# The lead-in of an mLSTM and FFN layer with its roundings on GpSimd and low gate weights last, and the turns of g and h later from chunk 4 on

## The reference

```python
h  = recurrence(layernorm(x) @ W + b)            # W is 256 x 1024: gates i, f, o and z
x1 = x + h / rms(h) * scale
u  = layernorm(x1)
out = x1 + u + 0.5 * (silu(layernorm_affine(u) @ w1 + b1) @ w2 + b2)
```

## Time and profile before

| | |
|---|---|
| time, median of 3 runs | 321.24 us (321.14 to 321.33) |
| the profiled execution | 321.89 us, span 320.0 us |
| busy share of the span | PE 95%, PEld 82%, DVE 84%, ACT 72%, POOL 37% |
| TensorE clock granted, mean | 0.989 of full speed |
| DMA | 13.12 MB on the main queue, 11.8% of 16 engines' span |

### The profile page before, as it was taken

One profiled execution on the slowest core, in us unless ns is written; L12 is line 12 of the kernel. 1 busy time (PEld: TensorE's weight loads), 2 busy tenths in 40 slices (PEclk: granted clock), 3 DMA queues, 4 the chain that ended last, 5 costly groups with the idle time before them and its releaser, 6 DMA issues.

```text
span 320.0 us, 4813 instructions
## 1 busy us (share of the span) xinstructions
PE 303.9 (95%) x1760; PEld 263.8 (82%) x1760; DVE 267.4 (84%) x474; ACT 229.7 (72%) x372; POOL 118.1 (37%) x126
## 2 busy tenths in 40 slices
...
GB/s 274 357 374 14 1 0 2 0 0 0 2 1 2 33 98 3 34 98 2 1 2 33 98 0 2 33 36 0 1 2 25 43 0 0 68 0 5 63 0 68
DMA packets 10951, 14.21 MB, mean 44 GB/s; under 512 B 688, under 2 KB 10160, under 8 KB 10672
## 3 DMA queue, kind: packets, MB, share of 16 engines
q1 hardware_dynamic: 10512, 13.12, 11.8%
q10 hardware_dynamic: 416, 0.79, 0.7%
...
## 4 chain that ended last, share of the span: by engine, by line
PE 45%; DVE 20%; issue 14%; POOL 12%; ACT 6%; DMA 3%; POOLq 0%; DVEq 0%; SPq 0%
PE mm_ps L221 7%; PE mm_ps L219 7%; PE mm_ps L220 7%; PE z_ps L220 6%; PE z_ps L219 6%; PE z_ps L221 6%; POOL rows L1034 3%; DVE rec L672 2%; DVE g L729 2%; DMA rows<-x 2%; POOL rec L1001 2%; DVE rows L737 2%; POOL g L1019 2%; DVE bn L742 2%; DVE rec L687 2%
## 5 line engine op out<-in xcount | busy, mean ns | idle before, releaser
L219 PE MATMUL z_ps<-w_hi,y_hi 128*128 128x256 f32 x248 | 71.3, 288 | 1.4 <-issue 1.4
L220 PE MATMUL z_ps<-w_lo,y_hi 128*128 128x256 f32 x248 | 70.4, 284 | 0.0
L221 PE MATMUL z_ps<-w_hi,y_lo 128*128 128x256 f32 x248 | 70.4, 284 | 0.0
L765 DVE TENSOR_TENSOR y_lo<-y,y_hi 128x512 fp32r<-128x512 f32 x64 | 43.2, 687 | 12.2 <-ACT y_hi L504 11.7
L501 ACT ACTIVATE y<-mm_ps,b_all 128x512 f32<-128x512 f32 x60 | 41.3, 688 | 13.4 <-PE mm_ps L288 9.8
L219 PEld LDWEIGHTS z_ps<-w_hi,y_hi 128*128 128x128 f32 x248 | 47.5, 191 | 1.9 <-issue 1.8
L220 PEld LDWEIGHTS z_ps<-w_lo,y_hi 128*128 128x128 f32 x248 | 47.2, 190 | 0.1
L221 PEld LDWEIGHTS z_ps<-w_hi,y_lo 128*128 128x128 f32 x248 | 47.1, 190 | 0.0
L1005 POOL TENSOR_TENSOR rrms<-meansq,minus_half 128x4 f32<-128x4 f32 x8 | 9.0, 1122 | 96.5 <-DVE meansq L723 96.5
L219 PE MATMUL mm_ps<-gt_hi,w_hi 128*128 128x512 f32 x108 | 43.2, 400 | 0.0
L220 PE MATMUL mm_ps<-gt_lo,w_hi 128*128 128x512 f32 x108 | 42.8, 396 | 0.0
...
## 6 DMA issues: line engine op xcount, KB each, us to landing
...
```

Of the source, the lines that this page charges most:

```text
L219: pe.matmul(dst, wh[w_at], ah[a_at], start=start, stop=False)
L220: pe.matmul(dst, wh[w_at], al[a_at], start=False, stop=False)
L221: return pe.matmul(dst, wl[w_at], ah[a_at], start=False, stop=stop)
L765: dve.tensor_tensor(y_lo[:, j], y[:, j % YBUFS], y_hi[:, j].bitcast(F32), ALU.subtract).then_inc(y_lo_done, 1)
```

## The change

The diff, cut to its core:

```diff
@@ @block.tensor
...
+            def first_two_gates():
+
+                x_hi, x_lo = xt(0)
+                f = [slice(GATE_ORDER[j] * P, GATE_ORDER[j] * P + P) for j in range(2)]
+                for k in range(KD):
+                    pe.wait_ge(wg_split_hi, k + 1)
+                    pe.wait_ge(xt_hi_done, k + 1)
+                    for j in range(2):
+                        pe.matmul(gate_bank(0, j), wg_hi[:, k, f[j]], x_hi[:, k], start=(k == 0), stop=False)
+                for k in range(KD):
+                    pe.wait_ge(xt_lo_done, k + 1)
+                    for j in range(2):
+                        pe.matmul(gate_bank(0, j), wg_hi[:, k, f[j]], x_lo[:, k], start=False, stop=False)
+                pe.wait_ge(wg_split_lo, KD)
+                for j in range(2):
+                    for k in range(KD):
+                        ins = pe.matmul(gate_bank(0, j), wg_lo[:, k, f[j]], x_hi[:, k], start=False,
+                                        stop=(k == KD - 1))
                     ins.then_inc(pre_done, 1)
...
-            gates(0, range(0, 5))
+            first_two_gates()
+            gates(0, range(2, 6))
             x_turned(1)
-            gates(0, range(5, GJ))
-            gates(1, range(0, 7))
+            gates(0, range(6, GJ))
+            gates(1, range(0, 5))
             x_turned(2)
-            gates(1, range(7, GJ))
-            gates(2, range(0, 2))
+            gates(1, range(5, GJ))
+            gates(2, range(0, 1))
             h_turned(0)
-            gates(2, range(2, GJ))
+            gates(2, range(1, GJ))
...
             for t in range(4, CHUNKS - 1):
                 gates(t, range(GJ))
+                fc2(t - 3, range(0, 2))
                 g_turned(t - 2)
-                fc2(t - 3, range(0, 2))
+                fc2(t - 3, range(2, TT))
                 x_turned(t + 1)
-                fc2(t - 3, range(2, TT))
+                fc1(t - 2, range(0, 2))
                 h_turned(t - 1)
-                fc1(t - 2, range(KF))
+                fc1(t - 2, range(2, KF))
             gates(7, range(GJ))
+            fc2(4, range(0, 2))
             g_turned(5)
-            fc2(4, range(TT))
+            fc2(4, range(2, TT))
...
@@ @block.scalar
-            act.preload_act_table_set("sigmoid_and_others")
+            act.preload_act_table_set("exp_and_others")
...
-            act.wait_ge(bias_ready, 3)
+            act.wait_ge(bias_ready, 5)
+
 
             gates(0, I_TILES)
-            act.preload_act_table_set("natural_log_exp_and_others")
             exp_i(0)
             act.preload_act_table_set("sigmoid_and_others")
-            gates(0, F_TILES)
+            gates(0, range(2, 6))
             x_high(1)
-            gates(0, range(4, 7))
-            act.wait_ge(w1_scaled, 1)
-            act.activation(w1_hi[:, 1], w1_f[:, 1], ACT.Copy).then_inc(w1_rounded, 1)
-            gates(0, range(7, GJ))
             x_normalised(2)
+            gates(0, range(6, GJ))
...
             gates(3, range(0, 1))
             square_sums(1)
-            gates(3, range(1, 4))
-            act.wait_ge(w2_scaled, 1)
-            act.activation(w2_hi[:], w2_f, ACT.Copy).then_inc(w2_rounded, 1)
-            gates(3, range(4, GJ))
+            gates(3, range(1, 2))
+            act.preload_act_table_set("sigmoid_and_others")
+            gates(3, range(2, GJ))
...
@@ @block.vector
-            for k in range(KD):
-                dve.wait_ge(wg_split_hi, k + 1)
-                dve.tensor_tensor(wg_lo[:, k], wg_raw[:, k], wg_hi[:, k].bitcast(F32), ALU.subtract
-                                  ).then_inc(wg_split_lo, 1)
...
+            dve.tensor_scalar(gate_bias[:, 2:4], col[:, 2:4], -1.0, None, ALU.mult).then_inc(bias_ready, 1)
+            dve.tensor_copy(gate_bias[:, 4:6], col[:, 6:8]).then_inc(bias_ready, 1)
+            dve.tensor_copy(gate_bias[:, 6:8], col[:, 4:6]).then_inc(bias_ready, 1)
+
+            ln1_sums(1)
             x_low(0)
...
-            dve.wait_ge(w1_scaled, 1)
-            dve.tensor_copy(w1_hi[:, 0], w1_f[:, 0]).then_inc(w1_rounded, 1)
             maximum(0, range(KD))
+            input_times_z(0)
             x_low(1)
...
-            y_low(0, range(2, 4))
-            for j in range(4, KF):
-                y_high(0, j)
-                y_low(0, range(j, j + 1))
-
-            ln1_sums(4)
+            y_low(0, range(2, KF))
+
+            ln1(4)
             mean_square(1)
-            ln1_means(4)
-            h_scaled(1)
             dve.wait_ge(w2_rounded, 1)
             dve.tensor_tensor(w2_lo[:], w2_f, w2_hi[:].bitcast(F32), ALU.subtract).then_inc(w2_ready, 1)
+            h_scaled(1)
             residual(1)
...
@@ @block.gpsimd
+            def y_high(c, j):
+                pool.wait_ge(silu_done, at(c, 8, j + 1))
+                pool.tensor_copy(y_hi[:, j], y[:, j % YBUFS]).then_inc(y_hi_done, 1)
+
...
             ln1_root(0)
+            for k in range(KD):
+                pool.wait_ge(wg_split_hi, k + 1)
+                pool.tensor_tensor(wg_lo[:, k], wg_raw[:, k], wg_hi[:, k].bitcast(F32), ALU.subtract
+                                   ).then_inc(wg_split_lo, 1)
             ln1_root(1)
             ln1_root(2)
-            input_times_z(0)
+            pool.wait_ge(w1_scaled, 1)
+            pool.tensor_copy(w1_hi[:], w1_f).then_inc(w1_rounded, 1)
...
             ln2_root(0)
             ln1_root(3)
+            for j in range(4, KF):
+                y_high(0, j)
+            pool.wait_ge(w2_scaled, 1)
+            pool.tensor_copy(w2_hi[:], w2_f).then_inc(w2_rounded, 1)
+            ln1_root(4)
             rms_root(1)
-            ln1_root(4)
             ln2_root(1)
```

More of the change, by code:

```diff
@@ L530, in _ @@
             exp_i(1)
+            x_high(2)
             act.preload_act_table_set("sigmoid_and_others")
[L532 to L536 removed]
+            gates(1, range(2, GJ))
+            gates(2, range(0, 1))
             square_sums(0)
[L538 removed]
+            gates(2, range(1, GJ))
             g_normalised(0)
@@ L875, in _ @@
             divisor(2)
-            numerators(2)
+            numerators(2, range(0, 1))
             g_low(1)
+            numerators(2, range(1, KD))
             newton(2)
```

122 lines of the change are left out of this document (68 added, 54 removed).

## The result

The changed kernel takes 325.78 us (324.85 to 326.67, 4 runs), the kernel before 321.19: a ratio of 1.0118, 95% interval 1.0092 to 1.0144. By that ratio it is slower by 1.2%; the two medians lie 4.6 us apart. I had forecast 318.0 and a range up to 320.9. The profiled execution took 326.67 us, 4.8 more than that of before (321.89), with a span of 324.6.

A forecast was written before the change was run, and what follows sets the result against it. PE (busy 95%) bounds the kernel, plus its waits and half-clock stretches. 0 to 90 us, +0.7 (to 1.5), -4.45 and 0 to +0.4 give -3.75 to -2.6, taken as -3.2: 318.0 us, range 315.6 to 320.9.

The forecast's parts named there:

- the lead-in's +0.4: Start of the kernel: POOL's wg_lo delays the first gate_bias and xt_lo, so PE comes 0.4 us later.
- rival C: Lead-in: POOL's wg_lo holds up DVE's scalings of chunk 0's x, once (320.4) or twice (322.8); chance 0.12.
- the 0 for the end of chunk 0's FFN: Up to 90 us: the 2.3 gained at fc2(0) is given back waiting at g_turned(1), sum about 0.
- 14 to 56 us, -1.15: Waits of 0.44 (xt_hi) and 0.72 (g of chunk 0) go; with the +0.4, PE is 0.75 earlier at fc1(0).
- POOL's rounding, 1.84: End of chunk 0's FFN: POOL's cast of w2 takes 1.84 us, between bounds of 1.68 and 3.24.
- The chain to g_turned(1): Chunk 0's FFN end: root stands behind w2_lo, g(1) is late, PE waits 2.25 us; half clock up to +1.7 possible.
- the 2.3: fc2(0) starts at 79.05 instead of 81.32 through earlier w2_lo: -2.3, counting the 0.75.
- Chunk 2's turn of h, +0.7: At h_turned(2), x_low(4) on a DVE 0.9 late delays PE: +0.7, with a fallen clock +1.5.
- Step 4, -4.45: Loop at t = 4: fc2 tiles ahead of g_turned(2) remove waits of 0.53 and 2.21 and the half clock (1.7).
- Steps 5 and 6, 0: Loop at t = 5 and 6: PE waited for nothing and g_high and g_low stay early enough: 0.
- Behind the loop I had 0 to +0.4: End of the kernel: a small remainder of 0 to +0.4 us.

The follow-up runs named there:

- first run: The kernel before with one edit, wg_lo subtracted by POOL at the place the changed kernel has it: 325.50 us, ratio 1.0130.
- third run: The changed kernel with POOL waiting for the four scalings of chunk 0's x before it subtracts wg_lo: 326.15 us, ratio 1.0148.
- thirteenth run: The changed kernel with wg_lo on DVE, x_low(0) right behind it, and the end of chunk 0's FFN as before: 320.22 us, ratio 0.9954.
- 2: The changed kernel with wg_lo subtracted by DVE right after x_normalised(0), as before: 324.47 us, ratio 1.0089.
- 5: The changed kernel with wg_lo on DVE and x_low(0) directly behind it, ahead of gate_bias and chunk 1's statistics: 323.99 us, ratio 1.0075.
- 6: The kernel before with the new loop, plus the changed kernel's end of chunk 0's FFN alone: 322.68 us, ratio 1.0024.
- 14: The changed kernel with shifted_bias in four pieces between tiles of gates(2) and g_normalised(0) earlier on ACT: 326.05 us, ratio 1.0144.
- the fourth: The kernel before with only the new order of the loop from t = 4 on: 318.87 us, ratio 0.9927.

## Why the prediction was wrong

- **The step that failed is the lead-in's +0.4; it was +4.7.** I let POOL's wg_lo run from 7.8 to 12.7 and asked what small operations it would hold. I took the scalings of x as over by then, without a row for when they begin. They began at 7.47 and ended at 8.85 in the kernel before, and the first half of wg_hi is there at 7.8, so POOL's first piece got in after the first scaling, and its second after the next. 4.0 of the 4.7 are this; the other 0.7 came in the first two gate tiles. The mechanism was in my own text as rival C, with its second price, "+4.8 (322.8)", and the row at 16.88 that speaks for it; I held against it that the scalings are mostly over by 7.8, which is the false reading. Even 322.8 is 3.0 short of the measured time, since the rest of that sum kept the 0 for the end of chunk 0's FFN. The first and third run show the mechanism. The Trainium skill (SBUF — State Buffer, Who interferes with whom) names tensor_scalar and copy among the operations that can hold or want the shared port; the rows 2.30 and 2.33 of the third run agree.
- **14 to 56 us, -1.15:** both waits did go in the changed kernel, and 0.6 came back by fc1(0) (4.7 late, then 4.1); PE was itself 4 us late there, so this does not show that the new order alone removes them. The half clock behind shifted_bias doubled, and on a lead-in that isn't late w1's rounding and `input_times_z(0)` make a new wait of 1.3, as the thirteenth run shows. I had no term for POOL's w1.
- **POOL's rounding, 1.84:** w1's, with nothing beside it, took 1.90 in the changed kernel; w2's took 2.35 and a y tile 1.08, beside DVE's y_low. The size was right and the sharing missing.
- **The chain to g_turned(1)** came as forecast: the root behind w2_lo, a wait of 2.25 predicted and 2.96 measured, and the half clock behind it, which I put at "up to +1.7" outside of the sum. It came in each run with that wait (the changed kernel, 2, 3, 5, 6, 14), and belonged into the sum. And the 2.3 that were to pay for it were 1.0 (4.6 late before fc2(0), 3.5 at it), since the six y_low took 7.05 us beside POOL's roundings, and since my chain let w2_lo start at the end of w2's rounding, though `ln1(4)`'s statistics stand between them in DVE's list; w2_lo itself took its 2.28. The edit as a whole was forecast at 0 and cost 3.4; in the sixth run it cost 1% against the fourth.
- **Chunk 2's turn of h, +0.7:** no wait. PE was later than DVE by then.
- **Step 4, -4.45:** right in size; -4.7 in the changed kernel and -4.5 in the fourth. But 1.7 of it is the half clock behind the wait at 127.57, and the first run had that wait without it: against such an execution the step is worth less.
- **Steps 5 and 6, 0:** right up to 262. Behind the loop I had 0 to +0.4, and it was +1.3, waits for y_lo.

The sum by the measured terms, in profiled executions: +4.7 - 1.2 + 4.4 - 4.7 + 1.3 = 4.5; the spans lie 4.6 apart.
